# A wide cross attention taken two slots at a time, with its running maximum in two rows

## The reference

```python
kv = jnp.einsum('bmc,cf->bmf', context, Wkv)      # context 8 x 1601 x 256
k, v = jnp.split(kv, 2, axis=-1)
k = jnp.concatenate((nk, k), axis=-2)             # 1602 keys with the learned one
v = jnp.concatenate((nv, v), axis=-2)
q = q * scale                                     # q from x, 16 heads of 64
sim = jnp.einsum('bhid,bhjd->bhij', q, k)
attn = jax.nn.softmax(sim, axis=-1)
out = jnp.einsum('bhij,bhjd->bhid', attn, v)      # then Wout and a layer norm
```

## Time and profile before

| what | value |
|---|---|
| median of three runs | 5413.99 us |
| the profiled execution's own time | 5408.82 us |
| its span (first to last instruction) | 5407.0 us |
| PE busy, whole span | 4232.4 us (78%) |
| DVE busy | 3490.8 us (65%) |
| ACT busy | 2440.3 us (45%) |
| POOL busy | 1297.6 us (24%) |
| first and last scores of the changed stage | 929.7 and 2851.3 us |

### The profile page before, as it was taken

How to read it: one execution, slowest core, us unless ns; L and a number is a source line. 1 busy time by engine, 2 the same in 40 slices (tenths; PEclk the granted TensorE clock), 3 DMA queues, 4 the chain that set the end, 5 groups by cost and what they waited for, 6 DMA issues and landing times. The chain is left out here.

```text
span 5407.0 us, 77657 instructions
## 1 busy us (share of the span) xinstructions
PE 4232.4 (78%) x29425; PEld 2213.8 (41%) x29507; DVE 3490.8 (65%) x5371; ACT 2440.3 (45%) x3320; POOL 1297.6 (24%) x963
## 2 busy tenths in 40 slices
PE   5630695999999999999994995894996586888872
PEld 3530234555555555555552332342443342222221
DVE  5469443676666667676665444566774456888867
ACT  2110241665565656565562222442564244777651
POOL 0000300455555555555553600000000000000000
PEclk5575797999999999999996997996997597999986
DMA  0010001000000000000001305314550315223200
GB/s 12 1 56 0 0 0 54 1 13 1 13 1 13 13 1 13 1 13 1 1 1 50 123 0 125 60 27 68 79 85 16 78 31 91 52 45 52 45 6 8
DMA packets 141075, 168.77 MB, mean 31 GB/s; under 512 B 19498, under 2 KB 110396, under 8 KB 139892
## 3 DMA queue, kind: packets, MB, share of 16 engines
q1 hardware_dynamic: 137812, 162.78, 14.4%
q0 software_dynamic: 1728, 1.08, 0.2%
q10 hardware_dynamic: 1184, 0.12, 0.0%
HBM read 126.36 MB, written 34.55 MB: 30 GB/s over the span
## 5 line engine op out<-in xcount | busy, mean ns | idle before, releaser
L2785 POOL TENSOR_TENSOR arena<-arena 128x512 f32<-128x512 f32 (+1 forms) x768 | 1094.9, 1426 | 889.1 <-ACT arena L2741 849.8
L2251 ACT ACTIVATE arena<-ps 128x1024 f32<-128x1024 f32 (+1 forms) x688 | 703.3, 1023 | 324.9 <-PE ps L2176 314.3
L2832 DVE TENSOR_TENSOR arena<-arena 128x1024 f32<-128x1024 f32 (+1 forms) x448 | 655.2, 1463 | 81.3 <-ACT arena L2768 81.3
L2269 DVE TENSOR_REDUCE arena<-ps 128x2 f32<-128x826 f32 (+1 forms) x576 | 564.6, 980 | 172.6 <-PE ps L2122 164.4
L2734 ACT ACTIVATE arena<-ps 128x1024 f32<-128x1024 f32 (+1 forms) x448 | 432.2, 965 | 435.9 <-PE ps L2660 435.8
L2808 DVE TENSOR_TENSOR arena<-ps,arena 128x512 f32<-128x512 f32 (+1 forms) x768 | 529.0, 689 | 98.4 <-ACT arena L2734 85.3
L2660 PE MATMUL ps<-arena 64*128 64x256 f32 (+1 forms) x3328 | 477.2, 400 | 105.9 <-DVE arena L2808 105.2
L2122 PE MATMUL ps<-arena 48*128 48x413 bf16 (+3 forms) x1920 | 435.6, 333 | 127.5 <-DVE arena L2269 65.9
L2674 PE MATMUL ps<-arena 128*64 128x256 f32 (+1 forms) x3328 | 460.3, 394 | 7.3 <-ACT arena L2741 7.2
L2644 PE MATMUL ps<-arena 128*128 128x256 f32 (+1 forms) x1664 | 462.1, 400 | 0.0
L2741 ACT ACTIVATE arena<-arena 128x1024 f32<-128x1024 f32 (+1 forms) x448 | 442.0, 987 | 15.5 <-DVE arena L2832 15.5
(11 more groups left out here) (639 smaller groups left out, 5880.3 us busy)
## 6 DMA issues: line engine op xcount, KB each, us to landing
arena<-ctx_parts SPq DMA_DIRECT2D x96, 200.1 KB
arena<-ctx_parts SPq DMA_DIRECT2D x192, 100.1 KB
arena<-in_ctx_feat SPq DMA_DIRECT2D x8, 1601.0 KB, 6.5
arena<-diff_att_stack SPq DMA_DIRECT2D x64, 192.0 KB, 5.7
arena<-in_ctx SPq DMA_DIRECT2D x16, 768.0 KB
ctx_parts<-arena SPq DMA_DIRECT2D x24, 400.2 KB, 3.7
arena<-in_w SPq DMA_DIRECT2D x1, 6416.0 KB, 17.7
arena<-in_ctx_feat SPq DMA_DIRECT2D x8, 800.5 KB, 6.1
```

Source lines behind the costliest of these rows:

```text
L2251: act.activation(self.prob[0:rows, u % 3, :], self.ps[0:rows, 2 * (u % 2):2 * (u % 2) + 2, :].rearrange("p n c -> p (n c)"), ACT.Exp).then ...
L2269: ins = dve.tensor_reduce(dst[:, :, j // 2], self.ps[:, 4:6, 0:hi - lo], AX.X, ALU.max)
L2785: pool.tensor_tensor(acc[0:rows, u % 2, :], before, sc[0:rows, u % 2, t, :], ALU.add).then_inc(added, 1)
L2832: dve.tensor_tensor(x, x, mb[0:rows, u % 2, None, :].to_broadcast([rows, n, 2 * S]), ALU.subtract).then_inc(sub_done, 1)
```

## The change

The loop goes over two slots at a time (a **pair**): PE does the scores of both, then the values of both, then all ring work of both. A turn now stands first in the ring work of its pair and a bcast last, both in the pair that holds k = 1. The running maximum has two rows of `top`, one for even and one for odd units, so that the first tile of unit u waits for the turn of u-2 and no more for that of u-1. ACT does the copies of both slots, then two exponentials, then the ring. DVE now does the two subtractions first, then the maxima of both slots of the same pair (which it did one slot later before), then the reduction of a turn, and at a unit's end reciprocal and product. Sums stand one slot later. The work itself is the same.

```diff
-        self.first, self.end = -self.STEPS, self.SLOTS + self.LAG + 4
+        self.first, self.end = -self.STEPS - 1, self.SLOTS + self.LAG + 8
...
     def ring_of(self, s):
...
+        early, keys, late = [], [], []
+        for x in (s, s + 1):
+            u, k = divmod(x, self.STEPS)
+            if u + 1 < self.UNITS and k == 0:
+                keys.append(("q", u + 1))
+            if 0 <= x < self.SLOTS and x % 14 < len(self.tiles):
+                keys.append(("v", x // 14, x % 14))
+            if u + 1 < self.UNITS and k in self.CHUNK_AT:
+                keys.append(("k", u + 1, self.CHUNK_AT[k]))
+            if k == 1 and 0 <= u - 1 < self.UNITS:
+                early.append(("turn", u - 1))
+                late.append(("bcast", u - 1))
...
+        return early + keys + late
+
+    def pair(self, s, lag=0):
+
+        return [(x - lag, *self.unit(x, lag)) for x in (s, s + 1) if self.unit(x, lag)]
...
-        top = st.sb("top", [P, 2 * S])
+        top = st.sb("top", [P, 2, 2 * S])
...
-            for s in range(plan.first, plan.end):
-                if plan.unit(s):
-                    scores(s, *plan.unit(s))
-                if plan.unit(s, plan.LAG):
-                    values(s - plan.LAG, *plan.unit(s, plan.LAG))
+            for s in range(plan.first, plan.end, 2):
+                for slot in plan.pair(s):
+                    scores(*slot)
+                for slot in plan.pair(s, plan.LAG):
+                    values(*slot)
                 for key in plan.ring_of(s):
...
-                done = plan.unit(s, plan.LAG + 1)
-                if done and done[1] == plan.STEPS - 1:
-                    u = done[0]
+                for u in plan.ended(s, plan.LAG + 2):
                     pe.wait_ge(added, last_tile * (u + 1))
...
-                if plan.unit(s, plan.LAG - 1):
-                    u, k = plan.unit(s, plan.LAG - 1)
+                for x, u, k in plan.pair(s, plan.LAG - 2):
...
-                    act.wait_ge(sub_done, s - plan.LAG + 2)
...
+                    act.wait_ge(sub_done, x + 1)
...
-            for s in range(plan.first, plan.end):
-                if plan.unit(s, 1):
-                    u, k = plan.unit(s, 1)
-                    dve.wait_ge(s_copied, s)
+            for s in range(plan.first, plan.end, 2):
+                for x, u, k in plan.pair(s, plan.LAG - 2):
...
+                    if k == 0:
+                        wait_copied(dve, ("bcast", u))
...
+                for x, u, k in plan.pair(s):
+                    dve.wait_ge(s_copied, x + 1)
                     for t in plan.tiles_of(k):
...
                         if t == 0:
-                            if u:
-                                dve.wait_ge(ring_ready, plan.index["turn", u - 1] + 1)
+                            if u >= 2:
+                                dve.wait_ge(ring_ready, plan.index["turn", u - 2] + 1)
```

More of the change, by code:

```diff
@@ L2521, in __init__ @@
         self.chunks = list(zip(cut[:-1], cut[1:]))
-        self.first, self.end = -self.STEPS, self.SLOTS + self.LAG + 4
+        self.first, self.end = -self.STEPS - 1, self.SLOTS + self.LAG + 8
         self.index, self.act_count, self.dve_count = {}, {}, {}
         n = a = d = 0
-        for s in range(self.first, self.end):
+        for s in range(self.first, self.end, 2):
             for key in self.ring_of(s):
@@ L2544, in ring_of, with ended @@
     def ring_of(self, s):
[L2546 to L2561, removed]
+        early, keys, late = [], [], []
[10 more added lines that the diff above has]
+                late.append(("bcast", u - 1))
+            last = x - self.LAG - 5 - 6
+            if last >= 0 and last % (self.STEPS * HP) == self.STEPS * (HP - 1):
+                late.append(("out", last // (self.STEPS * HP)))
+        return early + keys + late
+    def pair(self, s, lag=0):
+        return [(x - lag, *self.unit(x, lag)) for x in (s, s + 1) if self.unit(x, lag)]
+    def ended(self, s, lag):
+        return [u for _, u, k in self.pair(s, lag) if k == self.STEPS - 1]
 def stage4(env):
@@ L2693, in _ @@
                         for j in range(4):
-                            ins = pe.transpose(ps[:, bank, j * P:(j + 1) * P], top[:, j * P:(j + 1) * P], ident[:, :])
+                            ins = pe.transpose(ps[:, bank, j * P:(j + 1) * P], top[:, key[1] % 2, j * P:(j + 1) * P],
+                                               ident[:, :])
                         ins.then_inc(ring_ready, 1)
@@ L2722, in _ @@
             act.wait_ge(null_moved, 32)
-            for s in range(plan.first, plan.end):
-                if plan.unit(s):
-                    u, k = plan.unit(s)
+            for s in range(plan.first, plan.end, 2):
+                for x, u, k in plan.pair(s):
                     n = len(plan.tiles_of(k))
                     rows = tiles[2 * k][1]
-                    act.wait_ge(st_ready, s + 1)
+                    act.wait_ge(st_ready, x + 1)
                     if u >= 2:
-                        act.wait_ge(pv_done, s - 2 * plan.STEPS + 1)
+                        act.wait_ge(pv_done, x - 2 * plan.STEPS + 1)
                         act.wait_ge(added, last_tile * (u - 2) + plan.tiles_of(k)[-1])
-                    src = ps[0:rows, 2 + 2 * (s % 2):4 + 2 * (s % 2), 0:n * S].rearrange("p e (j q) -> p e j q", j=n)
+                    src = ps[0:rows, 2 + 2 * (x % 2):4 + 2 * (x % 2), 0:n * S].rearrange("p e (j q) -> p e j q", j=n)
                     dst = sc[0:rows, u % 2, 2 * k:2 * k + n, :].rearrange("p j (e q) -> p e j q", e=2)
                     act.activation(dst, src, ACT.Copy).then_inc(s_copied, 1)
-                if plan.unit(s, plan.LAG - 1):
-                    u, k = plan.unit(s, plan.LAG - 1)
+                for x, u, k in plan.pair(s, plan.LAG - 2):
                     n = len(plan.tiles_of(k))
                     rows = tiles[2 * k][1]
-                    act.wait_ge(sub_done, s - plan.LAG + 2)
-                    x = sc[0:rows, u % 2, 2 * k:2 * k + n, :]
-                    act.activation(x, x, ACT.Exp).then_inc(exp_done, 1)
+                    act.wait_ge(sub_done, x + 1)
+                    e = sc[0:rows, u % 2, 2 * k:2 * k + n, :]
+                    act.activation(e, e, ACT.Exp).then_inc(exp_done, 1)
                 for key in plan.ring_of(s):
@@ L2793, in _ @@
             ins.then_inc(null_k_ready, 1)
-            for s in range(plan.first, plan.end):
-                if plan.unit(s, 1):
-                    u, k = plan.unit(s, 1)
-                    dve.wait_ge(s_copied, s)
+            for s in range(plan.first, plan.end, 2):
+                for x, u, k in plan.pair(s, plan.LAG - 2):
+                    n = len(plan.tiles_of(k))
+                    rows = tiles[2 * k][1]
+                    if k == 0:
+                        wait_copied(dve, ("bcast", u))
+                    e = sc[0:rows, u % 2, 2 * k:2 * k + n, :]
+                    dve.tensor_tensor(e, e, mb[0:rows, u % 2, None, :].to_broadcast([rows, n, 2 * S]), ALU.subtract
+                                      ).then_inc(sub_done, 1)
+                for x, u, k in plan.pair(s):
+                    dve.wait_ge(s_copied, x + 1)
                     for t in plan.tiles_of(k):
                         rows = tiles[t][1]
-                        got = ps[0:rows, 2 + 2 * ((s - 1) % 2):4 + 2 * ((s - 1) % 2), t % 2 * S:(t % 2 + 1) * S]
-                        most = top[0:rows, :].rearrange("p (e q) -> p e q", e=2)
+                        got = ps[0:rows, 2 + 2 * (x % 2):4 + 2 * (x % 2), t % 2 * S:(t % 2 + 1) * S]
+                        most = top[0:rows, u % 2, :].rearrange("p (e q) -> p e q", e=2)
                         if t == 0:
-                            if u:
-                                dve.wait_ge(ring_ready, plan.index["turn", u - 1] + 1)
+                            if u >= 2:
+                                dve.wait_ge(ring_ready, plan.index["turn", u - 2] + 1)
                             ins = dve.tensor_copy(most, got)
```

## The result

The changed kernel takes **5542.35 us** (median of four runs, 5538.23 to 5551.63) against 5415.05 us before (four runs). The ratio is 1.024, 95% interval 1.0222 to 1.0259: slower by 127 us. The direction and the mechanism were forecast, but only 65 us of it. The time lies in the range of 5400 to 5570 us, but above the 5440 to 5530 us of A, the forecast itself. The profiled execution after takes 5551.63 us, 143 us more than the one before.

A forecast was written before the change was run, and what follows sets the result against it. PE, 94.5% busy, was taken as the bound. For two units -3.3 - 3.1 + 5.9 + 0.7 = +0.2 us, +6 us in all; half clock added 73 less 13, giving 5480 us on the median's scale, range 5400 to 5570.

The forecast's parts named there:

- A: The forecast itself: PE waits behind the turn and half clock follows, 5440 to 5530 us; chance 0.57.
- The removed wait: Scores no longer wait for DVE's maximum behind the turn: two waits of 1.67 us go, -3.3 us for two units.
- PE's own time: PE enters scores, values and ring work 7 times and no more 14: -3.1 us for two units.
- The wait behind the turn: A ring item behind the turn waits for its bank until DVE's reduction: 3.5 and 2.4 us, +5.9 for two units.
- The small waits: Ring items wait for a copy behind ACT's two exponentials: about +0.7 us for two units.
- The clock: New PE waits bring half clock: two in three of 64 at 1.7 us, +73 us, 13 off for idle time.
- rival D: Worse: DVE subtractions slowed beside POOL's additions, and longer half clock: 5592 us, either alone 5525 to 5550; chance 0.15.
- B: The same PE waits behind the turn but the clock holds: 5415 us, from 5400 to 5430; chance 0.18.
- C: Faster: a pair's second scores and ring items cost PE less and the clock holds: 5385 us; chance 0.10.

The follow-up runs named there:

- two_rows_alone: The kernel before with only the running maximum in two rows, slots one by one as before: 5289.05 us, ratio 0.9803 to the kernel before.
- reduce_early: The changed kernel with DVE's reduction of a turn between the subtractions and the maxima of its pair: 5244.52 us, ratio 0.9715 to the kernel before.
- product_late: The changed kernel with reciprocal and product of a unit's end one pair later on DVE: 5290.09 us, ratio 0.9781 to the kernel before.
- filled_waits: The changed kernel with matmuls on zero weights in PE's waits behind each turn, output unchanged: 5414.01 us, ratio 1.0015 to the kernel before.
- wait_longer: The kernel before with DVE's reduction of a turn ahead of a unit's first two maxima: 5472.38 us, ratio 1.0136 to the kernel before.
- filled_long_only: The changed kernel with zero-weight matmuls only in the 3.49 us waits, the 2.28 us waits left idle: 5450.94 us, ratio 1.0081 to the kernel before.
- changed_again: The changed kernel without any edit, run again beside the kernels with added matmuls: 5529.30 us, ratio 1.0229 to the kernel before.
- the shifts: Two runs of the changed kernel with two or four zero-weight matmuls per two units where PE is busy: 5513.64 and 5557.80 us.
- shifted_small: The changed kernel with two zero-weight matmuls per two units where PE is busy, away from the waits: 5513.64 us, ratio 1.0201 to the kernel before.

## Why the prediction was wrong in its size

**The removed wait.** Counted at -3.3 us for two units, 105 us in all; measured alone in two_rows_alone, -113 us. Right.

**PE's own time.** Counted at -3.1 us for two units, 99 us. PE's busy time at full clock fell from 1816 us (1921.6 less 106 idle) to 1733 (1872.8 less the 140), **83 us**. Two slots of values are as counted (1.88 us against 1.89). Two slots of scores are cheaper (1.93 us against 2.03), so they save 34 us where 19 were counted. The ring work is dearer than counted: it was to save 0.8 + 0.45 for two units, 40 us, and saved some 10. Grouping didn't make its items cheaper, as the timeline of PE in the change shows:

```profile
1774.75 1.13 PE L2652 MATMUL ps<-arena 128*128 128x256 f32 x4
1775.72 1.51 PE L2644 MATMUL ps<-arena 128*128 128x400 f32 x4
1777.06 1.03 PE L2652 MATMUL ps<-arena 128*128 128x256 f32 x4
```

Start to start a v takes 0.97 us and a k behind it, with another v next, 1.34 us, at full clock. That is what they took before.

**The wait behind the turn.** Counted at 3.5 and 2.4 us (0.2 of the 3.5 ahead of the scores), 189 us in all; measured 3.49 and 2.27, **180 us** in all. The reduction was counted to start at 8.2 us and PE to go on at 9.0; 8.36 and 9.10 were measured. The bank rule and DVE's queue are the mechanism: reduce_early and product_late shorten that queue in two ways and both take most of the wait away.

**The small waits.** Counted at 0.7 us for two units, 22 us. All idle time but the two waits came to some 8 us (2061 less 1873 busy is 188, less 180). This and the smaller saving cancel, which is luck. At full clock the sum was +6 us; the stage gives -83 - 105 + 180 + 8 = 0, and filled_waits measured +0.15%, 8 us, with interval 0 to 0.3%.

**The clock.** This is the step that failed, as a term too small: "I take two in three at 1.7". The mechanism was right, since filled_waits shows that all of the loss is half clock brought by idle time. But nearly every wait brought it, 60 stretches in the stage where 43 were counted, which adds 17 x 1.7 = 29 us. And 28 of them lasted 6.8 us, behind the long waits, the longer of the two lengths that I had read and set aside for rival D, which adds 28 x 1.7 = 48 us. The term was counted at 73 us less 13 for idle time, and is 73 + 29 + 48 less 10, **140 us**, in the profiled execution.

The share of two in three had no row behind it: in the prediction's own count the clock fell at all nine idle times. The length had three examples, two short and one long, and I took the short one for all. The experiments show why such a count is uncertain: of waits of 2.2 to 2.6 us in this stage 24 of 63 (wait_longer), 24 of 31 (filled_long_only), 28 of 31 (the change) or 25 of 31 (changed_again) brought half clock. Why 6.8 us follow 28 of the long waits when the short ones stand between them, and only 5 of 30 when these are filled, isn't settled; the shifts show only that the length of the waits isn't all.

**The rivals.** B (the clock holds) is refuted; with its clock filled_waits gives its time. C's cheaper second slot of scores did show, 1.93 - 1.06 = 0.87 us, but its cheaper ring items didn't, and the clock didn't hold. D's subtractions beside POOL didn't come (2.76 us for two, as counted), but its longer half clock did; that half of D alone had been priced at 5525 to 5550, where the time lies. The Trainium skill's advice (TensorE: Matmul & The Clock Gate, "Why this matters for your kernels"), no idle gaps of more than about 3 us, is too wide for this kernel: 2.2 us were enough in 24 of 63 cases, while waits of 1.67 us never did it in 63; at the stage's end, beside other idle time, one of 1.66 us did.

**A better version.** reduce_early, the change with the reduction ahead of the maxima, at 0.9715 of the kernel before and 0.991 of two_rows_alone (0.9715 / 0.9803). Two thirds of its gain is the second row of `top`; the pairs, with the reduction early, give the last 0.9%.

## What to carry to other kernels

When work is grouped into larger blocks on one engine, look at what then stands in front of the one short instruction that frees a shared bank: here a 0.68 us reduction behind 8 us of DVE's queue made PE wait, and putting it ahead of 2.9 us of maxima which nobody needed yet was worth 5%. Price an idle time of PE of over 2 us, in a stage like this one, with the half clock behind it, 1.7 or 3.4 us of work each time, and take as the range all and none of them: which ones bring it hangs on more than their length. And try the parts of a change alone; one array row more was worth 2% without any regrouping.

## What the runs showed of the hardware

- Idle times of 2.20 us in a stage that is otherwise full brought half clock in 24 of 63 cases (wait_longer), of 2.3 to 2.6 us in 24, 25 and 28 of 31 (filled_long_only, changed_again, the change), and of 3.48 us in all 30 (the change). Of 1.67 us none of 63 did it (the kernel before), of 0.64 and 0.9 us none either (reduce_early, product_late), but a single one of 1.79 us did (product_late).
- The stretches of half clock in the stage lasted 3.4 or 6.8 us. Adding 0.85 us of matmuls per 65 us, away from the waits, cut what they cost from 130 to 88 us (changed_again, shifted_small).
- Matmuls on weights of zeros in the waits kept the clock at 1.00 (filled_waits), as real work without waits did (two_rows_alone). That is a way to tell a loss by the clock from a loss by the wait itself: the order stays and only the idle time goes.
